# A gated-delta-rule attention kernel with experts: the first tile's key pairs in two PSUM banks, zeros for their halo corrections, and a later wait for constants

## The reference

```python
def short_conv(x, w):
    Kc = w.shape[-1]
    xp = jnp.pad(x, ((0, 0), (Kc - 1, 0), (0, 0))).transpose(0, 2, 1)
    y = lax.conv_general_dilated(xp, w[:, None, :], (1,), 'VALID', feature_group_count=w.shape[0])
    return jax.nn.silu(y.transpose(0, 2, 1))

q = short_conv(x @ Wq, conv_q).reshape(Bx, Tx, H, DK)
k = short_conv(x @ Wk, conv_k).reshape(Bx, Tx, H, DK)
v = short_conv(x @ Wv, conv_v).reshape(Bx, Tx, H, DV)
```

## Time and profile before

| what | us |
|---|---|
| median of 3 runs | 2949.16 |
| the profiled execution: its own time | 2968.65 |
| the profiled execution: span of its records | 2967.0 |
| TensorE matmuls busy | 2337.4 (79%) |
| VectorE busy | 2039.3 (69%) |
| ScalarE busy | 1251.2 (42%) |
| GpSimd busy | 1156.4 (39%) |
| mean granted TensorE clock | 0.95 of full speed |

### The profile page before, as it was taken

How to read it: one execution, slowest core, us unless ns; L and a number is a source line. 1 busy time by engine, 2 the same in 40 slices (tenths; PEclk the granted TensorE clock), 3 DMA queues, 4 the chain that set the end, 5 groups by cost and what they waited for, 6 DMA issues and landing times. The chain is left out here.

```text
span 2967.0 us, 93101 instructions
## 1 busy us (share of the span) xinstructions
PE 2337.4 (79%) x36510; PEld 1690.4 (57%) x36542; DVE 2039.3 (69%) x3917; ACT 1251.2 (42%) x3093; POOL 1156.4 (39%) x1152
## 2 busy tenths in 40 slices
PE   3344299999995788787878879788787887989786
PEld 3333189999982455464655646456464554646545
DVE  4333522223223888888888888888888888888885
ACT  0000034444332554444555545554455544555543
POOL 3443344444442243343524425243252433425233
PEclk9999899999997999999999989999899999989998
DMA  4334422222220010101101010010101101011010
GB/s 135 109 111 145 168 68 73 71 73 72 71 66 19 25 30 13 37 6 35 31 13 29 15 36 25 17 30 15 35 9 33 30 13 38 6 35 31 13 29 10
DMA packets 105639, 135.01 MB, mean 46 GB/s; under 512 B 39360, under 2 KB 78816, under 8 KB 105056
## 3 DMA queue, kind: packets, MB, share of 16 engines
q0 software_dynamic: 23552, 61.38, 6.8%
q1 hardware_dynamic: 62448, 40.55, 5.3%
q10 hardware_dynamic: 19312, 28.33, 2.7%
HBM read 76.18 MB, written 54.00 MB: 44 GB/s over the span
## 5 line engine op out<-in xcount | busy, mean ns | idle before, releaser
L1388 DVE SCALAR_TENSOR_TENSOR att_cv<-att_psA,att_cw,att_cv 128x508 f32<-128x508 f32 (+2 forms) x672 | 468.1, 735 | 102.0 <-ACT att_cv L1226 101.3
L971 PE MATMUL att_psA<-att_xt,att_wqkv 128*128 128x512 f32 x896 | 436.1, 632 | 83.7 <-DVE att_cv L1394 33.9
L1684 POOL TENSOR_TENSOR att_Sd<-att_S,att_mst 128x1024 f32<-128x1024 f32 x128 | 243.6, 1903 | 539.0 <-DVE att_S L1488 539.0
L971 PEld LDWEIGHTS att_psA<-att_xt,att_wqkv 128*128 128x128 f32 x896 | 170.8, 201 | 290.0 <-issue 205.1
L1093 PE MATMUL att_psS<-att_W,att_ktok 128*128 128x128 f32 x2048 | 257.2, 279 | 37.2 <-ACT att_W L1289 29.4
L1093 PEld LDWEIGHTS att_psS<-att_W,att_ktok 128*128 128x128 f32 x2048 | 241.3, 193 | 49.9 <-ACT att_W L1289 34.5
L734 PE MATMUL moe_psHT<-moe_xT,moe_w1s 128*128 128x128 f32 x2176 | 268.7, 277 | 0.0
L744 PE MATMUL moe_psY<-moe_w,moe_hT 128*128 x1088 | 258.1, 380 | 0.0
L734 PEld LDWEIGHTS moe_psHT<-moe_xT,moe_w1s 128*128 128x128 f32 x2176 | 257.1, 194 | 0.2
L1671 POOL TENSOR_TENSOR att_qg<-tri_q,att_mst 128x512 f32<-128x512 f32 x32 | 34.1, 1067 | 562.5 <-DMA att_mst<-token_stats 559.1
L701 DVE TENSOR_TENSOR moe_y<-moe_psY,moe_b2b 128x256 f32<-128x256 f32 x136 | 57.8, 425 | 271.8 <-PE moe_psY L744 161.6
(11 more groups left out here) (242 smaller groups left out, 4613.4 us busy)
## 6 DMA issues: line engine op xcount, KB each, us to landing
expert_out<-moe_y POOLq DMA_DIRECT2D x136, 128.0 KB
route_x_in<-in_L_attn_x_dram SPq DMA_DIRECT2D x64, 128.0 KB, 3.9
xn_rows<-route_xn ACTq DMA_DIRECT2D x16, 512.0 KB, 3.8
xn_cols<-route_xnT ACTq DMA_DIRECT2D x16, 512.0 KB, 3.1
moe_w<-in_L_ffn_W_dram ACTq DMA_DIRECT2D x2, 4096.0 KB
att_xt<-xn_cols SPq DMA_DIRECT2D x16, 512.0 KB, 4.3
att_xr<-in_L_attn_x_dram SPq DMA_DIRECT2D x64, 128.0 KB
out_dram<-att_xr SPq DMA_DIRECT2D x256, 32.0 KB, 1.8
```

The costliest lines, as they stand in the source:

```text
L971: last = MM(pair_bank(j)[:, h, :], wqkv[:, c, (2 * j + h) * P:(2 * j + h + 1) * P], xt[:, c, :], start=(c == 0), stop=(c == DC - 1))
L1388: V.scalar_tensor_tensor(out=late, in0=by_lane(src[:, h, :])[:, :, 0:LT - d], scalar=cw[:, 2 * j + h, TAPS - 1 - d:TAPS - d], in1=late, op ...
L1684: G.tensor_tensor(new, old, bc(mst[:, par, c, 4 + 2 * two:6 + 2 * two, :], 3, DV), op=ALU.mult).then_inc(s["sd_done" if two else "sd_half" ...
```

## The change

- Pairs 1 and 3 of tile 0 are projected into bank pair C; pairs 0 and 2 stay in A. The waits follow: project (0, j) for j = 1 to 3 waits for taps of pair j - 2, and project (0, 4), which writes C, now waits for all four key pairs. All other tiles are as before.
- TensorE's wait for consts and masks moves from the front to behind project (0, 0) and project (0, 1). Its order becomes project 0, 1, decays 0, project 2, decays 1, project 3, 4.
- ScalarE's order in first() becomes tap3 0, tap3 1, silu 0, decays 0, tap3 2, silu 1, tap3 3, decays 1, silu 2, silu 3.
- GpSimd writes att_corr as zeros with two memsets, ahead of the constants, instead of computing the halos of tile 0. The halo semaphores are advanced accordingly. The memset of att_tails goes, and consts counts to 10.

```diff
@@ -812,7 +812,7 @@
         block = ctx.enter_context(nc.Block())
         passed = ctx.enter_context(nc.semaphore("att_passed"))
         masks = ctx.enter_context(nc.semaphore("att_masks"))
-        NCONST = 11
+        NCONST = 10
 
         def credits(eng, which):
             for n in names[which].split():
@@ -844,9 +844,11 @@
 
             return cv[:, j % 2]
 
-        def pair_bank(j):
-
-            return pA if j < KP or j % 2 else pC
+        def pair_bank(m, j):
+
+            if j < KP:
+                return pC if m == 0 and j % 2 else pA
+            return pA if j % 2 else pC
 
         def by_lane(ap):
 
@@ -948,8 +950,6 @@
         def _(pe):
             credits(pe, "tensor")
             pe.wait_ge(params, 16 * NPARAM)
-            pe.wait_ge(consts, NCONST)
-            pe.wait_ge(masks, 2)
             MM, TR = nc.tensor.matmul, nc.tensor.transpose
 
             def project(m, j):
@@ -957,8 +957,10 @@
                     pe.wait_ge(xt_loaded, 16 * m + 16)
                     wait(pe, "taps_done", PAIRS * m)
                 elif j < KP:
-                    wait(pe, "taps_done", PAIRS * m + j)
+                    wait(pe, "taps_done", PAIRS * m + j - (1 if m == 0 else 0))
                 elif j == KP:
+                    if m == 0:
+                        wait(pe, "taps_done", KP)
                     wait(pe, "o_sum", GROUP * m)
                     wait(pe, "t2_done", GROUP * m)
                     wait(pe, "oT_done", GROUP * m - 1)
@@ -968,7 +970,7 @@
                     wait(pe, "taps_done", PAIRS * m + j - 1)
                 for h in range(2):
                     for c in range(DC):
-                        last = MM(pair_bank(j)[:, h, :], wqkv[:, c, (2 * j + h) * P:(2 * j + h + 1) * P], xt[:, c, :], start=(c == 0), stop=(c == DC - 1))
+                        last = MM(pair_bank(m, j)[:, h, :], wqkv[:, c, (2 * j + h) * P:(2 * j + h + 1) * P], xt[:, c, :], start=(c == 0), stop=(c == DC - 1))
                 last.then_inc(s["proj_ready"], 1)
 
             def project_gate(m, c):
@@ -1160,10 +1162,12 @@
 
             def first():
                 project(0, 0)
+                project(0, 1)
+                pe.wait_ge(consts, NCONST)
+                pe.wait_ge(masks, 2)
                 decays(0, 0)
-                project(0, 1)
+                project(0, 2)
                 decays(0, 1)
-                project(0, 2)
                 project(0, 3)
                 project(0, 4)
                 after_keys(0, 0, None)
@@ -1221,9 +1225,9 @@
                 wait(act, "silu_done", PAIRS * m + j - 1)
                 dst = conv(j)
                 wait(act, "k_halo" if j < KP else "vq_halo", m + 1)
-                A(tails[:, 2 * j:2 * j + 2, :, :], pair_by_lane(pair_bank(j)[:, :, :])[:, :, :, LT - 3:LT], ACT.Copy).then_inc(s["tails_done"], 1)
+                A(tails[:, 2 * j:2 * j + 2, :, :], pair_by_lane(pair_bank(m, j)[:, :, :])[:, :, :, LT - 3:LT], ACT.Copy).then_inc(s["tails_done"], 1)
                 for h in range(2):
-                    last = A(dst[:, h, :], pair_bank(j)[:, h, :], ACT.Copy, scale=cw[:, 2 * j + h, TAPS - 1:TAPS])
+                    last = A(dst[:, h, :], pair_bank(m, j)[:, h, :], ACT.Copy, scale=cw[:, 2 * j + h, TAPS - 1:TAPS])
                 last.then_inc(s["tap3_done"], 1)
 
             def silu(m, par, j):
@@ -1325,14 +1329,14 @@
 
             def first():
                 tap3(0, 0, 0)
+                tap3(0, 0, 1)
+                silu(0, 0, 0)
                 decays(0, 0, 0)
-                silu(0, 0, 0)
-                tap3(0, 0, 1)
+                tap3(0, 0, 2)
+                silu(0, 0, 1)
+                tap3(0, 0, 3)
                 decays(0, 0, 1)
-                silu(0, 0, 1)
-                tap3(0, 0, 2)
                 silu(0, 0, 2)
-                tap3(0, 0, 3)
                 silu(0, 0, 3)
                 after_keys(0, 0, None)
 
@@ -1379,7 +1383,7 @@
 
                 i = TAP_OPS * (PAIRS * m + j)
                 wait(dve, "tap3_done", PAIRS * m + j + 1)
-                dst, src = conv(j), pair_bank(j)
+                dst, src = conv(j), pair_bank(m, j)
                 for d in range(1, TAPS):
                     for h in range(2):
                         if d > 1:
@@ -1610,16 +1614,19 @@
         def _(pool):
             credits(pool, "gpsimd")
             G = pool
+            G.memset(corr[:, 0:H, :, :], 0.0).then_inc(s["k_halo"], 1)
+            G.memset(corr[:, H:QKV, :, :], 0.0).then_inc(s["vq_halo"], 1)
+            for step in ("k_halo_step", "vq_halo_step"):
+                G.sem_inc(s[step], 4)
             G.memset(identb[:, :], 0.0).then_inc(consts, 1)
             G.memset(half[:, :], 0.5).then_inc(consts, 1)
             G.memset(mhalf[:, :], -0.5).then_inc(consts, 1)
-            G.memset(tails[:, :, :, :], 0.0).then_inc(consts, 1)
             G.memset(S[:, 0:2, :], 0.0).then_inc(consts, 1)
             G.memset(S[:, 2:4, :], 0.0).then_inc(consts, 1)
             G.memset(sel[:, :], 0.0).then_inc(consts, 1)
             G.memset(W[:, 0:4, :, :], 0.0).then_inc(consts, 1)
             G.memset(W[:, 4:8, :, :], 0.0).then_inc(consts, 1)
-            G.wait_ge(consts, 9)
+            G.wait_ge(consts, 8)
             G.memset(sel[:, 32:33], 1.0).then_inc(consts, 1)
             G.affine_select(out=identb[:, :], in_=identb[:, :], compare_op=ALU.not_equal, fill=1.0, base=0,
                             pattern=[[-1, P]], channel_multiplier=1).then_inc(consts, 1)
@@ -1707,8 +1714,6 @@
                 gather(f)
 
             def first():
-                key_halo(0)
-                value_query_halo(0)
                 decay_sums(0, 0, 0)
                 decay_sums(0, 0, 1)
                 read(0, 0, 0, 0)
```

## The result

The changed kernel takes 2927.7 us (median of 6 runs, 2923.2 to 2934.78) against 2949.17 (6 runs, 2947.27 to 2952.1): a ratio of 0.9925, 95% interval 0.9906 to 0.9943. The forecast was 2930, so the time is 2.3 us from it.

The account below looks back on a forecast made before the run. The opening was taken as bound by a relay of projection, ScalarE's copies and VectorE's taps, nothing saturated. Gains of 3.0 (start) and 20.7 (overlap) less 4.6 make 19.1: 2949.16 - 19.1 = 2930 us, range 2924 to 2937.

Parts of the forecast that it names:

- the milestone: Start of VectorE's second Y product in the opening: forecast at 937.4 instead of 956.54, 19.1 us gained.
- M: Time from issue of the first column load (att_xt) to VectorE's second Y product; forecast 19.1 us shorter.
- Start: First projection no longer waits for constants, only for parameters and att_xt: starts at about 900.5, 3.0 us gained.
- Zeros: Two memsets replace GpSimd's ten small halo products in the opening; the decay product moves up, gaining nothing by itself.
- Overlap: Two banks in turn: first projection to end of fourth pair's correction takes 25.7 us instead of 46.4, +20.7.
- Table loads: ScalarE's opening: five table loads for three, 1.28 us each, all hidden, one with 0.3 us to spare.
- Project (0,4): Waits for pair 3's correction at 926.2, no longer hidden; costs 5.8 us after TensorE stands still for 5.7.
- first rival: Pauses do not lower TensorE's clock: project (0,4) takes 3.60, keys come 2.2 us sooner, 2926 at best; chance 0.14.
- Keys: Key products behind project (0,4): start at 932.0 instead of 951.16, same 5.33 us, including 2.01 of "issue".
- The end: Later tiles: the opening's shift should come through to the kernel's end within about 3 us either way.
- R: Rest of the span from the second Y product to the end; the shift should pass through within about 3 us.
- The slower rival: Project (f,0) in later tiles meets the low clock, 3.1 us more each; 2977 with all 15; chance 0.03.

Follow-up runs that it names:

- wait_front: Changed kernel with TensorE's wait for constants and masks back at the front; 2791.28 us against 2809.87 for the kernel before on that chip, ratio 0.9942.
- wait_only: Kernel before with only TensorE's wait for constants and masks moved behind project (0,0); 2808.24 us against 2809.87 on that chip, ratio 1.0000.
- fewer_loads: Changed kernel with ScalarE doing decays 0 ahead of silu 0, three table loads instead of five; 2931.64 us, ratio 0.9920 to the kernel before.
- halo_products: Changed kernel with the first tile's halo corrections computed again by GpSimd from zeroed tails; 2788.15 us, ratio 0.9924 to the kernel before.
- warm_six: Changed kernel with 6 unused matmuls in TensorE's pause ahead of project (0,4); 2793.39 us, ratio 0.9922 to the kernel before.
- three_turns: Changed kernel with the first tile's pairs in banks A, C, S, A, C, three table loads, GpSimd's Sd products later; 2931.86 us, ratio 0.9920 to the kernel before.
- filled: Changed kernel with four unused matmuls per tile in TensorE's pause ahead of the query products; 2785.89 us, ratio 0.9903 to the kernel before.
- three_turns_filled: three_turns with the same four unused matmuls per tile ahead of the query products; 2781.46 us, ratio 0.9892 to the kernel before.
- before_again: The kernel before, run again unchanged on a second chip; 2809.74 us against 2809.87 there, ratio 0.9997.

## Why the prediction was right

The time, the milestone and the mechanism came out as forecast. That M met the forecast to 0.2 us (40.95 against 937.4 - 896.2 = 41.2) is luck: the relay was 0.6 us longer, project (0,4) 0.5 and the keys 0.4 us shorter than forecast, and M was 40.0 to 41.4 in the five executions whose opening should take the same time.

- *Start.* Forecast 4.3 us after the load's issue, measured 4.35. As a term of the sum (3.0) it is right: 7.28 us before, 4.35 after, 2.9 less. To put the wait back into the changed kernel costs more (wait_front: 3.8 to 4.8 at the milestone), as the mask has become slower there. By itself the term would not have held. In wait_only the same 3.2 us were worth 0.4: the correction fell into GpSimd's products, and TensorE's restarts took back more. The step "nothing in it gets longer" in the expectation of wait_only had no row under it; the 0.45 us of the first correction, between corrections of 0.18, was the sign that I passed over.
- *Zeros.* Nothing, confirmed within the scatter of M. That they bring GpSimd's decay product beside VectorE's mask, 0.7 us, was not foreseen and is covered.
- *Overlap.* Forecast 25.7 us from the first projection to the end of the fourth pair's correction, measured 921.61 + 0.18 - 895.48 = 26.3: the first projection took 6.53 instead of 5.85, the rest of the relay went to 0.1 us as worked out, pauses included (0, 0.98 and 0.28 for 0, 0.8 and 0.4). Without the earlier start it gave 14.8 us with its share of project (0,4) (wait_front), against 16.1 in the sum; the slower mask and a project (0,4) of 6.60 us account for 1.5.
- *Table loads.* Five, hidden; the rows' 1.28 us stands. By the price of the Trainium skill ("ScalarE: Activation LUTs", section "What ACT_TABLE_LOAD costs"), with a drain, M would have been 44, an estimate from that page (41.2 + 2.8); it was 41. The trace does not agree with the drain: the load at 912.93 is followed by the next activation 1.30 us later, and with two loads fewer M was no shorter (fewer_loads).
- *Project (0,4).* Forecast 5.8 behind a pause of 5.7, measured 5.32 behind 5.75 (5.11 to 6.66 in the other kernels with this pause), and 3.6 to 3.7 with the pause filled, which was the first rival's price. The clock was low there because of the pause.
- *Keys.* 5.33 forecast, 4.93 measured; the "issue" in their midst stayed (2.35 us).
- *The end.* The gain of M did reach the second tile whole. That it reaches the end to within 3 us I could not show with one run: R alone scatters by more than 10 us. The changed kernel twice and halo_products, -21.5, -21.0 and -21.7 us against the kernel before, say that it does, within intervals that are 11 us wide and more; the 2 us above M are inside them.
- *The slower rival* had a real mechanism, but the shift did not set it off. Project (f,0) took 5.3 to 5.4 us instead of 3.7 in 4 of 15 tiles, in the changed kernel (first row) and in the kernel before (second row) alike, in sum 62.2 against 62.4 us. That is 1.7 us for each, not 3.1. The larger variation from tile to tile is in the stretch around the query products, 6.5 to 9.1 us, and that one too came out no longer with the change.

```profile
2238.40 5.40 PE L973 MATMUL att_psA<-att_xt,att_wqkv 128*128 128x512 f32 x8 [2.46 <-DMA att_xt<-xn_cols]
```

```profile
2521.14 5.40 PE L971 MATMUL att_psA<-att_xt,att_wqkv 128*128 128x512 f32 x8 [2.39 <-DMA att_xt<-xn_cols]
```

What stays open: why gains of 2 to 5 us at the milestone (warm_six, three_turns) didn't show in the medians. Their intervals are 12 and 16 us wide, so the gains may simply be covered; that the later tiles take them back is not excluded.

## What to carry to other kernels

Where VectorE, ScalarE and TensorE hand one PSUM pair round, count the banks over the whole relay, the pair behind it included: the second pair took some 20 us out of the relay here and, being booked by the next pair as well, took 5 back, which a third pair of banks returned at the milestone. A filled pause can pass the low clock on to the next matmuls, so add up their times too before counting a gain. Before an instruction is moved to an earlier time, look at what GpSimd does there: an operation of 0.18 us can become one of 1.8. And in a kernel with pauses on TensorE compare a milestone of the trace, not only the median, as the pauses scatter the rest by more than such a change is worth.

## What the hardware showed

- A correction with two SBUF inputs on VectorE took 0.18, 0.45 or 1.82 us, ending with GpSimd's Sd products wherever it was longer (796.35 beside 796.31), and 0.18 again with these moved away.
- A mask of 0.60 us took 1.29 us with GpSimd's decay product of 1.05 us beside it, and 0.60 again with the halo products in between (halo_products).
- Project (0,4) took 5.1 to 6.7 us behind a pause of 5.7 us and 3.6 to 3.7 us (2.4 GHz throughout) with matmuls in the pause. Queries and gate behind pauses of 3.8 to 5 us had a mean granted clock of 0.50 to 0.62 in each stretch of over 8 us, of which there were 3 to 14 in 15 tiles, differently in each execution. With matmuls in that pause the clock was 1.00 in 8 of 15 stretches (filled) and 6 of 15 (three_turns_filled). An "issue" gap of 2.1 us among small query matmuls was followed by the low clock in one tile and not within the stretch in another.
- Project (f,0) took 3.7 us or 5.1 to 5.8 us: 1 to 4 slow ones of 15 without the filling ahead of the queries, 8 (filled) and 2 (three_turns_filled) with it.
- The kernel before took 2810, 2813 and 2956 us on three chips. Most of the difference is ahead of the attention stage (t0 775 to 779 us on two of the chips, 891 to 896 on the others), and 2 us in each tile (123.8 in before_again against 125.8).
